# Taking the two row tiles of a pair in one operation in the scores of a masked linear attention

## The reference

```python
# x (16, 1024, 512), adj (1024, 1024), Wq, Wk, Wv (512, 512), all float32
q, k, v = x @ Wq.T, x @ Wk.T, x @ Wv.T            # per batch
rel = adj.T * (q @ k.T)                           # (1024, 1024) per batch
rel = rel / norm(rel, axis=2, keepdims=True)
out = layernorm(x + rel @ v)                      # over the last axis, eps 1e-5
```

## Time and profile before

| What | us |
|---|---|
| median of three runs | 1972.1 (1971.42 to 1972.16) |
| the profiled execution | 1971.97 |
| its span | 1970.2 |
| PE busy | 1957.0 |
| DVE busy | 1531.9 |
| POOL busy | 957.8 |
| ACT busy | 762.5 |

### The profile page before, as it was taken

One profiled execution on the slowest core, in us unless ns is written; L12 is line 12 of the kernel. 1 busy time (PEld: TensorE's weight loads), 2 busy tenths in 40 slices (PEclk: granted clock), 3 DMA queues, 4 the chain that ended last, 5 costly groups with the idle time before them and its releaser, 6 DMA issues.

```text
span 1970.2 us, 28685 instructions
## 1 busy us (share of the span) xinstructions
PE 1957.0 (99%) x9857; PEld 1669.1 (85%) x9857; DVE 1531.9 (78%) x2085; ACT 762.5 (39%) x1288; POOL 957.8 (49%) x639
## 2 busy tenths in 40 slices
PE   8999999999999999999999999999999999999998
PEld 6888888888888888888888888888888888888887
DVE  8796877868778696787968779687796877868775
ACT  5433434335342352423424234342433424335341
POOL 5744536455354553446435374453644536455352
PEclk9999999999999999999999999999999999999999
DMA  5734343344524345343444333443434343344401
GB/s 188 314 134 165 144 167 115 144 154 154 186 92 149 142 157 184 122 151 118 157 175 160 128 139 133 172 153 128 160 128 170 144 155 127 144 154 152 185 26 64
DMA packets 80416, 292.22 MB, mean 148 GB/s; under 512 B 7441, under 2 KB 7441, under 8 KB 76305
## 3 DMA queue, kind: packets, MB, share of 16 engines
q1 hardware_dynamic: 80400, 292.06, 40.2%
HBM read 251.13 MB, written 40.89 MB: 148 GB/s over the span
## 4 chain that ended last, share of the span: by engine, by line
PE 97%; DVE 1%; POOL 1%; DMA 0%; issue 0%; SPq 0%; ACT 0%; POOLq 0%; DVEq 0%
PE banks L422 32%; PE banks L424 32%; PE banks L423 32%; DMA scr<-xT 0%; DVE aw L794 0%; DVE x_lo L755 0%; POOL scr L1063 0%; DVE yv L816 0%; POOL square_sum L1067 0%; POOL squares L1067 0%; SPq L344 0%; POOL scr L1072 0%; SPq L343 0%; POOL res L1075 0%; POOL res L1080 0%
## 5 line engine op out<-in xcount | busy, mean ns | idle before, releaser
L422 PE MATMUL banks<-yv 128*128 128x512 f32 x1024 | 399.8, 390 | 0.0
L424 PE MATMUL banks<-yv 128*128 128x512 f32 x1024 | 398.5, 389 | 0.0
L423 PE MATMUL banks<-yv 128*128 128x512 f32 x1024 | 398.5, 389 | 0.0
L1119 POOL TENSOR_TENSOR square_sum<-square_sum,squares 128x512 f32<-128x512 f32 x224 | 319.9, 1428 | 85.7 <-ACT squares L657 75.1
L422 PE MATMUL banks<-yv,x_hi 128*128 128x512 f32 x896 | 348.7, 389 | 0.5 <-DVE rel L857 0.5
L424 PE MATMUL banks<-yv,x_lo 128*128 128x512 f32 x896 | 348.6, 389 | 0.0
L423 PE MATMUL banks<-yv,x_hi 128*128 128x512 f32 x896 | 348.6, 389 | 0.0
L1136 POOL TENSOR_TENSOR rstd<-var_eps,minus_half 128x1 f32<-128x1 f32 x128 | 144.2, 1127 | 329.3 <-DVE var_eps L968 329.3
L423 PE MATMUL banks<-aw,x_hi 128*128 128x256 f32 x896 | 253.6, 283 | 0.0
L424 PE MATMUL banks<-aw,x_lo 128*128 128x256 f32 x896 | 253.5, 283 | 0.0
L422 PE MATMUL banks<-aw,x_hi 128*128 128x256 f32 x896 | 253.5, 283 | 0.0
(11 more groups left out here) (108 smaller groups left out, 3430.5 us busy)
## 6 DMA issues: line engine op xcount, KB each, us to landing
scr<-adj SPq DMA_DIRECT2D x128, 512.0 KB, 5.8
aw<-w_kept SPq DMA_DIRECT2D x16, 3584.0 KB, 11.1
aw<-a_kept SPq DMA_DIRECT2D x15, 3584.0 KB, 11.0
scr<-xT SPq DMA_DIRECT2D x32, 1024.0 KB, 7.1
res<-x SPq DMA_DIRECT2D x128, 256.0 KB, 2.7
out<-res SPq DMA_DIRECT2D x128, 256.0 KB, 2.0
a_kept<-aw SPq DMA_DIRECT2D x1, 3584.0 KB, 18.2
w_kept<-v_raw SPq DMA_DIRECT2D x3, 512.0 KB, 8.5
```

Of the source, the lines that this page charges most:

```text
L422: pe.matmul(bank_ap, l_hi, r_hi, start=first and i == 0, stop=False, skip_group_check=on)
L423: pe.matmul(bank_ap, l_hi, r_lo, start=False, stop=False, skip_group_check=on)
L424: mm = pe.matmul(bank_ap, l_lo, r_hi, start=False, stop=i == len(pairs) - 1, skip_group_check=on)
L1119: pool.tensor_tensor(square_sum[:, h, :], square_sum[:, h, :], squares[:, n % SQRING, :], ALU.add).then_inc(square_added, 1)
```

## The change

Adjacent banks become one operand of 128 by 1024, and so do the two tiles' blocks in `rel` and the two mask tiles (which lie side by side in `scr`). In stage S, ACT's copy, DVE's seven operations and POOL's mask take both tiles of a pair at once, wait for what the second tile needs, and raise their semaphores by 2. In ACT's order the copy of pair 0 stands where the copy of tile 0 stood, that of pair 1 where those of tiles 2 and 3 stood. PE's list, the squares, their additions, SP's list and stages Y, V and O are as before.

```diff
+        s_first_bank = [{"a": 6, "c": 0, "b": 2}, {"a": 4, "c": 6, "b": 0}]
+        def s_banks(pair, n):
+            return banks[:, s_first_bank[pair][n]:s_first_bank[pair][n] + 2, :]
+        def c_pair(block_name, pair):
+            first = 2 * pair + (HT if block_name[0] == "2" else 0)
+            half = int(block_name[1]) - 1
+            return rel[:, first:first + 2, half * BANK:(half + 1) * BANK]
+        def adj_pair(m, half):
+            return scr[:, adj_slot[m]:adj_slot[m] + 2, half * BANK:(half + 1) * BANK]
...
-            def s_copy(b, i):
-                act.wait_ge(s_done, s_count(b, 1, i))
-                act.activation(c21(i), s_bank[i // 2]["a"][i % 2], ACT.Copy).then_inc(s_p1, 1)
+            def s_copy(b, pair):
+                act.wait_ge(s_done, s_count(b, 1, 2 * pair + 1))
+                act.activation(c_pair("21", pair), s_banks(pair, "a"), ACT.Copy).then_inc(s_p1, 2)
...
                 s_copy(b, 0)
                 y_t1_block(b, 0)
-                s_copy(b, 1)
                 y_t1_block(b, 1)
                 y_last_block(b)
...
-                s_copy(b, 2)
-                s_copy(b, 3)
+                s_copy(b, 1)
...
             def s_blocks(b, pair):
-                a, bb, c = (s_bank[pair][n] for n in ("a", "b", "c"))
-                tiles = (2 * pair, 2 * pair + 1)
-                for i in tiles:
-                    dve.wait_ge(s_p1, b * HT + (i + 1))
-                    dve.wait_ge(s_done, s_count(b, 6, i))
-                    dve.tensor_tensor(c12(i), c[i % 2], c21(i), ALU.add).then_inc(s_u2, 1)
+                a, bb, c = (s_banks(pair, n) for n in ("a", "b", "c"))
+                t, last = 2 * pair, 2 * pair + 1
+                dve.wait_ge(s_p1, b * HT + (last + 1))
+                dve.wait_ge(s_done, s_count(b, 6, last))
+                dve.tensor_tensor(c_pair("12", pair), c, c_pair("21", pair), ALU.add).then_inc(s_u2, 2)
...
-                for i in tiles:
-                    dve.wait_ge(s_done, s_count(b, 4, i))
-                    dve.tensor_tensor(c21(i), c[i % 2], c21(i), ALU.add).then_inc(s_c21, 1)
-                for i in tiles:
+                dve.wait_ge(s_done, s_count(b, 4, last))
+                dve.tensor_tensor(c_pair("21", pair), c, c_pair("21", pair), ALU.add).then_inc(s_c21, 2)
+                for i in (t, last):
                     dve.wait_ge(adj_loaded[HT + i], b * DMA + DMA)
-                    dve.wait_ge(s_c21, b * HT + (i + 1))
-                    dve.tensor_tensor(c21(i), c21(i), adj_of(HT + i, 0), ALU.mult).then_inc(s_m21, 1)
+                dve.wait_ge(s_c21, b * HT + (last + 1))
+                dve.tensor_tensor(c_pair("21", pair), c_pair("21", pair), adj_pair(HT + t, 0), ALU.mult).then_inc(s_m21, 2)
...
-            def mask22(b, i):
-                pool.wait_ge(adj_loaded[HT + i], b * DMA + DMA)
-                pool.wait_ge(s_c22, b * HT + (i + 1))
-                pool.tensor_tensor(c22(i), c22(i), adj_of(HT + i, 1), ALU.mult).then_inc(s_m22, 1)
+            def mask22(b, pair):
+                for i in (2 * pair, 2 * pair + 1):
+                    pool.wait_ge(adj_loaded[HT + i], b * DMA + DMA)
+                pool.wait_ge(s_c22, b * HT + (2 * pair + 2))
+                pool.tensor_tensor(c_pair("22", pair), c_pair("22", pair), adj_pair(HT + 2 * pair, 1),
+                                   ALU.mult).then_inc(s_m22, 2)
```

More of the change, by code:

```diff
@@ L871, in s_blocks @@
                         y_lo_piece(b, B22, j, y_b22_raw[j])
-                for i in tiles:
+                for i in (t, last):
                     dve.wait_ge(adj_loaded[i], b * DMA + DMA)
-                    dve.wait_ge(s_done, s_count(b, 2, i))
-                    dve.tensor_tensor(c11(i), a[i % 2], adj_of(i, 0), ALU.mult).then_inc(s_m11, 1)
-                for i in tiles:
[L878 to L888, removed]
-                    dve.wait_ge(s_done, s_count(b, 4, i))
-                    dve.tensor_tensor(c21(i), c[i % 2], c21(i), ALU.add).then_inc(s_c21, 1)
-                for i in tiles:
-                    dve.wait_ge(adj_loaded[HT + i], b * DMA + DMA)
-                    dve.wait_ge(s_c21, b * HT + (i + 1))
-                    dve.tensor_tensor(c21(i), c21(i), adj_of(HT + i, 0), ALU.mult).then_inc(s_m21, 1)
@@ L896, in s_blocks @@
[L896 to L903, removed]
+                dve.wait_ge(s_done, s_count(b, 2, last))
+                dve.tensor_tensor(c_pair("11", pair), a, adj_pair(t, 0), ALU.mult).then_inc(s_m11, 2)
@@ new lines, in s_blocks @@
+                if pair == 0:
+                    dve.wait_ge(y_t1, b * 2 + 2)
+                    dve.wait_ge(y_split[B22], b * 2 + 2)
+                dve.wait_ge(s_done, s_count(b, 7, last))
+                dve.tensor_tensor(c_pair("22", pair), c, c_pair("21", pair), ALU.add).then_inc(s_r, 2)
+                dve.wait_ge(s_r, b * HT + (last + 1))
+                dve.wait_ge(s_done, s_count(b, 5, last))
+                dve.tensor_tensor(c_pair("22", pair), bb, c_pair("22", pair), ALU.add).then_inc(s_c22, 2)
@@ new lines, in s_blocks @@
+                dve.wait_ge(s_done, s_count(b, 4, last))
+                dve.tensor_tensor(c_pair("21", pair), c, c_pair("21", pair), ALU.add).then_inc(s_c21, 2)
+                for i in (t, last):
+                    dve.wait_ge(adj_loaded[HT + i], b * DMA + DMA)
+                dve.wait_ge(s_c21, b * HT + (last + 1))
+                dve.tensor_tensor(c_pair("21", pair), c_pair("21", pair), adj_pair(HT + t, 0), ALU.mult).then_inc(s_m21, 2)
+                dve.wait_ge(s_u2, b * HT + (last + 1))
@@ L905, in v_lo_piece @@
+                dve.wait_ge(s_done, s_count(b, 3, last))
+                dve.tensor_tensor(c_pair("12", pair), bb, c_pair("12", pair), ALU.add).then_inc(s_c12, 2)
+                dve.wait_ge(s_c12, b * HT + (last + 1))
+                dve.tensor_tensor(c_pair("12", pair), c_pair("12", pair), adj_pair(t, 1), ALU.mult).then_inc(s_m12, 2)
             def v_lo_piece(b, block, i, source):
@@ L1124, in s_blocks @@
                     if name == "m22" and i % 2 == 0:
-                        mask22(b, i)
-                        mask22(b, i + 1)
+                        mask22(b, i // 2)
                     if (name, i) not in firsts:
```

## The result

The changed kernel takes 1991.0 us (median of four runs, 1990.6 to 1991.5) against 1971.8 for the kernel before: 19.3 us more, a ratio of 1.0097 with the interval 1.0085 to 1.0110. The forecast was 1988.0, its range 1977 to 1993. The profiled execution took 1990.55, its span is 1988.4.

A forecast was written before the change was run, and what follows sets the result against it. The prediction took PE, 99% busy, as the bound, with a chain without slack delaying O by 1.00 us a batch; 16 batches made 16.0 us on the profiled 1971.97, so 1988.0 us, range 1977 to 1993.

The forecast's parts named there:

- What bounds the kernel: PE, 99% busy, bounds the time; at O's start a chain without slack already holds it by 0.1 to 0.2 us.
- Prices: Costs of the paired 128x1024 operations: 1.22 us on DVE, 1.06 on ACT, 2.41 for POOL's mask.
- What is merely later: Paired sums and copies in S end later but still in time for PE; no cost.
- Steps 1 to 5: End of pair 1: later sums, masks and additions put ACT's first copy for V at 1059.14, PE 0.34 us late.
- Steps 6 and 7: Additions end at 1062.13 instead of 1059.79, delaying DVE's low pieces; transposes start at 1064.35, 1.00 us late.
- the cover: Time between the end of POOL's additions of squares and the transposes, 3.6 us, which the change uses up.
- Step 8: Nothing behind the transposes takes up the delay: O starts 1.00 us late, with V's 0.34 inside it.
- Step 1: DVE's paired sum of block 22 ends at 1049.26, POOL's paired mask at 1051.75.
- A reason given among the rivals: Against all being hidden: the two paired masks take 1.1 us each out of POOL's time in any order.
- no change: Rival: all is hidden, additions end near 1061 and ACT's copy by 1058.8, time 1972 us; chance 0.10.
- faster: Rival: DVE's shorter list brings a low piece of v forward, PE's gap at O goes, 1970.4 us; chance 0.03.
- the third rival: POOL's T1 and T4 pieces in pair 0 also late, 0.3 to 0.6 us a batch more, 1993 to 1998; chance 0.14.

The follow-up runs named there:

- e4: Kernel before, with ACT's second eight small copies moved behind two high pieces of v: 1969.4 us, ratio 0.9987.
- e1: Changed kernel with all ten operations paired in pair 0 and none in pair 1: 1972.1 us, ratio 1.0002.
- e12: Kernel before with only POOL's mask of block 22 paired, in pair 1: 1975.8 us, ratio 1.0019.
- e11: Kernel before with only block 22's last sum on DVE and its mask on POOL paired, in pair 1: 1983.0 us, ratio 1.0057.
- e5: Changed kernel with each of ACT's copies of product 1 of V put one square earlier: 1991.4 us, ratio 1.0098.
- e8: Changed kernel with DVE's masks of blocks 21 and 12 in pair 1 tile by tile again: 1988.2 us, ratio 1.0083.
- e7: Changed kernel with block 22's last sum and mask in pair 1 tile by tile again: 1972.5 us, ratio 1.0003.
- e10: Changed kernel without pairing block 22's last sum and mask in pair 1, with the eight small copies moved later: 1969.9 us, ratio 0.9990.

## Why the prediction was right

- **What bounds the kernel**: right. PE's own list is 120.8 us a batch in every kernel measured, and each change of the time is idle time of PE. The gap in the matmuls of the earlier trace rows, read as a wait on a chain without slack, was one: e4 takes it away.
- **Prices**: 1.23 on DVE (taken 1.22), from banks and from SBUF, 1.03 on ACT (taken 1.06), 2.41 on POOL (taken 2.41). DVE makes eight operations a tile in S, not seven as stated ahead of the prediction (five sums and three masks), so a batch has sixteen paired ones, not fourteen. They save more than the 2.2 a batch that the prediction gave as the most: 4.3 (411.5 us in all before, 342.9 after), of which 2.7 on the masks of blocks 21 and 12, which POOL now holds back less often. Nothing hangs on this, as PE waits for none of it.
- **What is merely later**: right. No wait of PE in S, and e1 shows that pair 0 costs nothing.
- **Steps 1 to 5**: right to a tenth or two. The copy ends at 1059.33 (forecast 1059.14), and the weight load behind it is 0.47 late (forecast 0.34). That the profile shows a wait of 0.34 at the matmul is a coincidence, for it leaves out the last 0.11.
- **Steps 6 and 7**: right in kind. The additions were put at 1062.13 and end at 1062.30, the transposes at 1064.35 and start at 1064.50. Their distance, 2.22 by the forecast, is 2.20. The prediction also called 3.6 us the cover, which is over twice what could be used up, but its steps did not use that number.
- **Step 8**: right. The delay passes on undiminished (e12, e11, after), and the wait in V lies inside it (e5). The "over 0.4 to spare" of PE's later waits in V was too much: e5 shows 0.14 of waiting there once the 0.45 of the first wait is gone, so some 0.3 were to spare.
- **The size** was off: 16 us against 18.2 in the span and 19.3 in the medians. The term that was too small is the 1.00 a batch, which is 1.14. Step 1 has nearly all of it. DVE's sum of block 22 starts 0.07 later than where the sum of its second tile had stood (1048.11 against 1048.04), and POOL's mask starts 0.15 behind the end of the sum (forecast 0.08): the mask ends at 1051.89, forecast 1051.75. Further on, a DVE operation that waits for the one just before it was given 0.03 and takes 0.13 (line 904 starts at 1061.06, line 900 ended at 1059.70 + 1.23 = 1060.93). What these have in common stands in the last section. The last 1.1 us of the medians are in no trace: the profiled execution of after lies 0.5 below the median of its kernel, that of before 0.2 above, and after has 2.2 us outside its span, 0.4 more than before.
- **A reason given among the rivals** was wrong. I held that the two paired masks take 1.1 each from POOL in any order, so that all could not be hidden. The masks of one tile had taken nearly as much: with them by tile again (e8) the additions end only 0.23 earlier. In e7 the masks are paired, the additions end 1.2 later than before, and all is hidden. What decided was the late start behind block 22.
- **The range** was said to leave out under 0.2. By the prediction's own chances it leaves out 0.27: 0.10 for no change, 0.03 for faster, and 0.14 for the third rival, which begins where the range ends.
- **The rivals**: none came. The third (T4 pieces late) had the right margin and stayed on the safe side of it.

## What to carry to other kernels

Where the busiest engine has no idle time, joining two operations of another engine bought nothing here (e1, e10), and it makes the first half of the result as late as the second: ask who was using that half early. Follow the half through every list in which it stands, here a ring of two buffers, an adder, an engine's hand-written order, up to the first place where the saturated engine has a gap of even 0.1 us; a chain that ends in such a gap passes every delay on. And when an item is taken out of a chain, its worth is the idle time of the others for it (0.68 here, and 0.58 came of it), not its length (1.9).

## What the runs showed of the hardware

- The wait that the profile shows at a matmul is shorter than what it costs. In V a matmul starts 0.12 behind its own weight load; the first one behind the wait for ACT's copy starts together with it, both at 1068.25. So the gap ahead of it shows 0.34 to 0.35, and 0.10 more come ahead of the next matmul (0.08 in O: 0.31 us from 1083.54 to 1083.85 where 0.23 is usual). PE is 0.45 late from there on (median over the batches), as the weight load was (0.46).
- An operation over two adjacent PSUM banks costs what one from SBUF of that size costs: 1.23 us on DVE for 128x1024 in both cases.
- A wait that stands in an instruction of its own costs a hand-over more. The trace's semaphore records show it: the 256 paired operations of DVE, which raise their semaphore by 2, carry no wait themselves; ahead of 239 of them stands a waiting instruction within 0.15 us, as a rule 0.07 before the operation. The other 869 of DVE's operations of this kind (tensor with tensor), which raise theirs by 1, all carry one. Behind such a waiting instruction line 904 starts 0.13 behind the end of line 900, and POOL's paired mask 0.14 behind DVE's sum, where the mask of one tile took 0.08. In e8 the mask of one tile waits for the same paired sum but raises its semaphore by 1, and it starts 0.03 behind the end:

```profile
1058.75 1.22 DVE L911 TENSOR_TENSOR rel<-banks,rel 128x1024 f32<-128x1024 f32 x1 [1.50 <-PE banks L445]
1060.01 0.69 DVE L916 TENSOR_TENSOR rel<-rel,scr 128x512 f32<-128x512 f32 x1
```

This fits the missing 0.14 a batch of the prediction. That pairs which raise their semaphore by 1 would give it back is not tested. An operation that waits for nothing starts about 0.08 before the end of the one ahead.
